# Local attention of a transformer kernel: three steps of 4, 4 and 3 query chunks per head pair in place of four of 3, 2, 3 and 3

## The reference, cut to what matters

```python
for i in range(6):
    x = attn_layer(shift_tokens(x), Wqkv[i], q_scale[i], k_scale[i], Wo[i]) + x
    x = ffn_layer(shift_tokens(x), ...) + x

def attn_layer(x, Wqkv, qs, ksc, Wo):
    q, k, v = split(x @ Wqkv)               # 16 heads of 64
    q, k = l2norm(q) * qs, l2norm(k) * ksc  # then rotary tables with a scale
    sim = 8 * q @ k.T                       # only keys 0 to 32 tokens back, in windows of 32
    return softmax(sim) @ v @ Wo
```

## Time and profile before

| | |
|---|---|
| Median of 3 runs | 5900.51 us (5897.06 to 5904.95) |
| Span of the profiled execution | 5900.4 us |
| Its own time beside the span | not given apart; the runs' median is 0.1 us above the span |
| PE busy | 5495.2 us, 93% |
| DVE busy | 4294.8 us, 73% |
| ACT busy | 4093.6 us, 69% |
| POOL busy | 2762.7 us, 47% |
| DMA queue 1 | 76.74 MB, 4.6% of 16 engines |

### The profile page before, as it was taken

The page is one execution under the profiler, slowest core; times in us unless marked ns, Lnnn a source line. Parts: engine busy times, 40 slices in busy tenths (PEclk is TensorE's granted clock), DMA queues, the critical chain, the costliest instruction groups (busy, mean ns, idle before and its releaser), DMA issues. The chain is left out here.

```text
span 5900.4 us, 159891 instructions
## 1 busy us (share of the span) xinstructions
PE 5495.2 (93%) x60258; PEld 3949.3 (67%) x60258; DVE 4294.8 (73%) x6692; ACT 4093.6 (69%) x7768; POOL 2762.7 (47%) x2483
## 2 busy tenths in 40 slices
PE   8998986899999999999998899899999999999998
PEld 3334443678777777777776333677777778777776
DVE  7876654777777777777775886777777777777775
ACT  5774654677777777777775577677777777777775
POOL 1101100566655665556663110566556666556663
PEclk8997998899999999999999899999999999999999
DMA  0000000100000000000000000100000000000000
GB/s 13 2 2 6 2 3 8 36 17 16 19 14 19 17 16 20 15 18 16 16 21 10 4 2 2 36 17 16 20 13 19 17 16 21 16 17 16 17 20 18
DMA packets 128857, 87.46 MB, mean 15 GB/s; under 512 B 33332, under 2 KB 121936, under 8 KB 128056
## 3 DMA queue, kind: packets, MB, share of 16 engines
q1 hardware_dynamic: 128056, 76.74, 4.6%
HBM read 68.96 MB, written 1.05 MB: 12 GB/s over the span
## 5 line engine op out<-in xcount | busy, mean ns | idle before, releaser
L1733 POOL TENSOR_TENSOR cross<-raw,tab_b 128x512 f32<-128x512 f32 x768 | 998.1, 1324 | 304.6 <-ACT raw L1600 301.8
L737 DVE TENSOR_REDUCE arena<-PS 128x1 f32<-128x512 f32 (+3 forms) x1408 | 828.4, 646 | 216.4 <-PE PS L550 130.5
L1739 POOL CAST kT_b<-kT 128x512 bf16<-128x512 f32 x384 | 311.9, 812 | 1318.2 <-ACT kT L1656 1318.2
L688 ACT ACTIVATE arena<-PS 128x1024 f32<-128x1024 f32 (+1 forms) x704 | 668.4, 968 | 203.1 <-PE PS L573 126.3
L1853 DVE TENSOR_TENSOR oT<-PS,rec_den 128x288 f32<-128x288 f32 (+1 forms) x768 | 326.2, 425 | 635.2 <-ACT rec_den L1634 635.2
L1824 DVE TENSOR_TENSOR rot<-PS,tab_a 128x512 f32<-128x512 f32 x768 | 521.9, 686 | 227.9 <-PE PS L1451 133.8
L1406 PE MATMUL PS<-qT,kT 64*128 64x96 f32 x8448 | 660.6, 287 | 0.0
L1626 ACT ACTIVATE PT<-PS 128x576 f32<-128x576 f32 (+1 forms) x768 | 468.7, 610 | 257.9 <-PE PS L1406 245.3
L1600 ACT COPY raw<-PS 128x512 f32<-128x512 f32 x768 | 447.1, 589 | 285.5 <-PE PS L1451 244.8
L1840 DVE TENSOR_TENSOR rot<-rot,cross 128x1024 f32<-128x1024 f32 x384 | 613.4, 1597 | 17.8 <-POOL cross L1733 17.4
L1847 DVE TENSOR_TENSOR rot<-rot,inv_norm 128x1024 f32<-128x1024 f32 x384 | 578.6, 1507 | 10.6
(11 more groups left out here) (260 smaller groups left out, 13084.0 us busy)
## 6 DMA issues: line engine op xcount, KB each, us to landing
w_qk<-in_w_pairs SPq DMA_DIRECT2D x196, 128.0 KB, 2.1
w_v<-in_w_pairs SPq DMA_DIRECT2D x100, 128.0 KB, 2.2
w_o<-in_w_out_pairs SPq DMA_DIRECT2D x192, 64.0 KB, 1.9
xs<-staged SPq DMA_DIRECT2D x24, 224.0 KB, 2.6
w<-in_L_ffn_W SPq DMA_DIRECT2D x12, 341.0 KB
q_parts<-max_rows SPq DMA_DIRECT2D x192, 2.0 KB
V<-in_c_E SPq DMA_DIRECT2D x2, 896.0 KB, 8.3
w<-in_L_ffn_W SPq DMA_DIRECT2D x24, 64.0 KB
```

Source lines behind the costliest of these rows:

```text
L688: nc.scalar.activation(PT[u % 6].rearrange("p (a n) -> p a n", a=2)[:, :, first_q:512], PS[:, 2 * (u % 2):2 * (u % 2) + 2, first_q:512], A ...
L737: nc.vector.tensor_reduce(maxima[:, 2 * m + h, qt, kh:kh + 1], bank[:, 0:keys_of(qt, kh)], AX.X, ALU.max).then_inc(bank_free, 1)
L1733: nc.gpsimd.tensor_tensor(dst[:, :, :, o:o + 32], src[:, :, :, other:other + 32], tab[:, :, o:o + 32].unsqueeze(2).broadcast_to([128, 8, 2 ...
```

## The change

Three steps of 4, 4 and 3 chunks take the place of four of 3, 2, 3 and 3. Tiles for exp and denominators grow to four chunks; the number of steps in the semaphore counts becomes NS = 3; the row group of a mask product is looked up for each chunk, since a step now has chunks of both. Slot 4 follows slot 3 with no step between them, on PE, ACT and DVE. The last step's values, denominators and quotient stay at the start of the next position.

```diff
-        PT = [own(f"PT{m}", [128, 2, 3 * QC]) for m in range(2)]
-        log_den = own("log_den", [128, 3 * QC])
-        rec_den = [own(f"rec_den{m}", [128, 3 * QC]) for m in range(2)]
+        PT = [own(f"PT{m}", [128, 2, 4 * QC]) for m in range(2)]
+        log_den = own("log_den", [128, 4 * QC])
+        rec_den = [own(f"rec_den{m}", [128, 4 * QC]) for m in range(2)]
...
-        STEPS = ((0, (0, 1, 2)), (0, (3, 4)), (1, (5, 6, 7)), (1, (8, 9, 10)))
+        STEPS = (range(0, 4), range(4, 8), range(8, 11))
+        NS = len(STEPS)
...
                 def scores(l, b, p, r, s):
-                    g, chunks = STEPS[s]
+                    chunks = STEPS[s]
...
-                    need(pe, exp_done, r * 4 + s)
+                    need(pe, exp_done, r * NS + s)
                     for i, c in enumerate(chunks):
+                        g = int(c in GROUPS[1])
...
@@ position of PE
                     if oo:
-                        values(r - 1, 3, (p + 6) % 8)
+                        values(r - 1, NS - 1, (p + 6) % 8)
...
-                    for s in range(3):
+                    for s in range(NS - 1):
                         if bb:
                             scores(l, b, p, r, s + 1)
...
                             values(r, s, (p + 7) % 8)
                         late(l, b, p, s + 2)
+                    late(l, b, p, 4)
...
@@ position of DVE
-                    for s in range(1, 4):
+                    for s in range(1, NS):
                         late(l, b, p, s + 1)
-                        if bb and s < 3:
+                        if bb and s < NS - 1:
                             quotients(r, s, (p + 1) % 2)
+                    late(l, b, p, 4)
```

More of the change, by code:

```diff
@@ L1423, in values @@
                 def values(r, s, pair):
-                    chunks = STEPS[s][1]
-                    need(pe, exp_done, r * 4 + (s + 1))
-                    need(pe, o_done, r * 4 + s)
+                    chunks = STEPS[s]
+                    need(pe, exp_done, r * NS + (s + 1))
+                    need(pe, o_done, r * NS + s)
                     for i, c in enumerate(chunks):
@@ L1455, in max_rows @@
                 def max_rows(l, b, p):
-                    need(pe, exp_done, (item(l, b, p) - 1) * 4)
+                    need(pe, exp_done, (item(l, b, p) - 1) * NS)
                     for g in range(2):
@@ L1466, in outputs @@
                     if f == 0:
-                        need(pe, o_done, (item(l, b, p) - 1) * 4)
+                        need(pe, o_done, (item(l, b, p) - 1) * NS)
                         need(pe, wo_in, (item(l, b, p) - 1) * 16)
@@ L1622, in exps @@
                 def exps(r, s):
-                    n = QC * len(STEPS[s][1])
-                    need(act, st_full, r * 4 + (s + 1))
-                    need(act, pv_full, r * 4 + (s - 1))
+                    n = QC * len(STEPS[s])
+                    need(act, st_full, r * NS + (s + 1))
+                    need(act, pv_full, r * NS + (s - 1))
                     nc.scalar.activation(PT[s % 2][:, :, 0:n], PS[:, 4:6, 0:n], ACT.Exp).then_inc(exp_done, 1)
                 def denominators(r, s):
-                    n = QC * len(STEPS[s][1])
-                    need(act, pv_full, r * 4 + (s + 1))
+                    n = QC * len(STEPS[s])
+                    need(act, pv_full, r * NS + (s + 1))
                     nc.scalar.activation(log_den[:, 0:n], PS[:, 7, 0:n], ACT.Ln).then_inc(ln_done, 1)
-                    need(act, ln_done, r * 4 + (s + 1))
-                    need(act, o_done, r * 4 + (s - 1))
+                    need(act, ln_done, r * NS + (s + 1))
+                    need(act, o_done, r * NS + (s - 1))
                     nc.scalar.activation(rec_den[s % 2][:, 0:n], log_den[:, 0:n], ACT.Exp, scale=-1.0).then_inc(den_done, 1)
@@ L1681, in position @@
                     if oo:
-                        denominators(r - 1, 3)
+                        denominators(r - 1, NS - 1)
                     if a:
@@ L1849, in quotients @@
                 def quotients(r, s, par):
-                    chunks = STEPS[s][1]
+                    chunks = STEPS[s]
                     lo, n = QC * chunks[0], QC * len(chunks)
-                    need(dve, den_done, r * 4 + (s + 1))
+                    need(dve, den_done, r * NS + (s + 1))
                     nc.vector.tensor_tensor(oT[par][:, lo:lo + n], PS[:, 6, 0:n], rec_den[s % 2][:, 0:n], ALU.mult).then_inc(o_done, 1)
@@ L1918, in position @@
                     if oo:
-                        quotients(r - 1, 3, p % 2)
+                        quotients(r - 1, NS - 1, p % 2)
                     if bb:
```

## The result

The changed kernel takes 5867.8 us (median; 5859.9 to 5870.5) against 5901.0: a ratio of 0.994, 95% interval 0.9926 to 0.9954, or 33 us less. I had forecast 100 us less. The sign and most terms of the sum were right; one wait was not in it, and one effect, the clock, was some fifteen times as large as I priced it.

A forecast was written before the change was run, and what follows sets the result against it. The prediction took PE, busy 93% of the span, as the bound. From about 5900 us it took 83 + 93 saved less 33, 13, 28 and 2 of new costs, 100 us: 5800 us, range 5740 to 5870.

The forecast's parts named there:

- Cheaper steps: On PE, three steps instead of four save a step's fixed part, 0.43 us a pair, 83 us over 192 pairs.
- Rival 3: Only what is removed is saved: just the ones product has a fixed part per step, 15 us; 5868 us, chance 0.12.
- Waits that go: PE's values products stop waiting for quotients (65 us) and mask products mostly for an exp (28 us): 93 us saved.
- (a): Slot 4: PE waits to turn K1 and q1 behind DVE's normalise, at positions 1, 2 and 4: 33 us lost.
- (b): Position 3: slots 3 and 4 back to back load ACT with copies, 0.6 us each time: 13 us lost.
- (c): Position 7: next batch's first query-key product waits 2.3 us for X1 at 12 places, loop returns already idle: 28 us lost.
- (d): Granted clock falls to half after one in eight of 12 gaps, 1.25 us each: 2 us lost.
- ACT loses an Exp, a Ln and an Exp per pair ... I cost it at nothing: ACT's and DVE's fewer instructions per pair shorten no path, because PE is the bound: 0 us.
- Waits that come: The prediction's list of new PE waits and their clock cost after the change, terms (a) to (d): 33, 13, 28 and 2 us.
- Rival 1: Slower: DVE's chain at slot 4 runs longer as the sine add stretches beside POOL; 5944 us at 1.2 us more, chance 0.08.
- rival 2: More gain: new waits (a), (b) and (c) overlap or don't come; 5725 us, chance 0.12.

The follow-up runs named there:

- four_again: Four steps of 3, 3, 3, 2 chunks put back in the changed kernel with the first two edits, sine's reorder and X1 turned in slot 2: 5929.9 us.
- sine: Changed kernel with the first two edits, plus DVE's sine add for the second half moved ahead of quotient 0: 5761.9 us, ratio 0.9759.
- stat: Changed kernel with ACT's two layer-norm rstd instructions moved from slot 4 of position 2 to slot 0 of position 3: 5813.6 us, ratio 0.9851.
- before_both: Kernel before, with its four steps, given the first two edits: 5888.8 us, ratio 0.9978.
- the first two edits: On the changed kernel, stat's rstd move, and Q0 and Q1 waiting for X0 alone (alone 5836.0 us); both together 5799.3 us.

## Why the prediction was right and wrong

- **Cheaper steps, 83 us:** right. 0.44 a pair, 84 us. The fixed part is in all four groups: in the medians the mask products take 0.44, 0.35 and 0.27 us for 4, 3 and 2 chunks, the scores 1.06, 0.84 and 0.62, the values 0.71, 0.55 and 0.38, the ones products 0.74, 0.59 and 0.42. That leaves some 0.09, 0.18, 0.05 and 0.1 beside the chunks, and four_again gives it back. Rival 3, that only the ones product has it, is out. The page "TensorEngine Tiling (Array Packing)" of the Trainium skill, section "Instruction Overhead", counts about 60 cycles for each matmul, and the estimate from it was 19 us, less than a quarter of what the rows show. That the rest comes from the changes between the groups' tile shapes is likely, but no run tried it.
- **Waits that go, 93 us:** right. 60 us at the values and 30 at the mask products.
- **(a) Turning K1 and q1, 33 us:** right in mechanism and about right in size. The profile has 27 us of idle time for it (47.0 less the 19.6 that was there), but a wait also costs the overlap with the product before it, 0.1 to 0.15 us. From start to start position 2 loses 0.5, position 4 0.75 and position 1 0.1, against 0.55, 0.8 and 0.15, and position 7 loses 0.45, which I had not listed: 1.8 x 22 = 40. sine shows the cause and gives 37 back.
- **(b) ACT's copies at position 3, 13 us:** about right in size. N1's product and the second maxima product of position 4 take 0.5 and 0.2 us more, 15 us; it was N1 and the banks after it that waited, and not Q0. No experiment tried it.
- **(c) X1, 28 us:** 12 gaps of 1.76, 21 us, with the 0.33 to 0.45 ahead of them counted under (a): the forecast 2.3 split in two. But I called the 8 loop returns hidden, and they grew by 1.0 us each: **8 us missed**.
- **(d) The clock, 2 us:** wrong, and by far. Slow stretches are in 19 places against 1 before, 7 at loop returns, 6 at X1 and 6 at position 3 behind the waits for banks. Over their 12 products each costs about 1.2 us (0.21 from start to start against 0.12, and a little more), 22 us, but the lower clock lasts on into the groups behind them. By all of PE's work it is (78 - 14) / 2 = 32 us: **30 us missed**. PE's busy time agrees, for it fell by only 50 us where the steps alone take 84 away. I had taken a share of one in eight from gaps of 2.2 us and used it for others. The share was misread too: I judged seven returns by their first product. In the kernel before, the clock fell at three of the eight, 1.4 us after PE had gone on at the second return of the earlier trace rows:

```profile
2110.52:2111.92 1.40, 1.40 (x12) 1.40 (x12) 0.47 (x1) 0.40 (x1) 0.00 (x0) 1.00 0.08 18
...
2112.00:2115.00 3.00, 3.00 (x20) 1.40 (x19) 1.97 (x3) 1.10 (x3) 2.76 (x1) 0.50 0.01 3
```

  By the changed kernel's trace half of the X1 gaps pay, and waits of 1.1 us behind another of 0.5 do too.
- **What was not in the sum:** the step "ACT loses an Exp, a Ln and an Exp per pair ... I cost it at nothing" looked at ACT's work and not at its queue. "Waits that come" walks through slot 4 for PE and DVE, and through ACT's copies only at position 3; it left out ACT's wait for DVE's moments at the head of slot 4 in position 2. **38 us missed**, shown by stat and by the control before_both.

The sum with measured terms is 84 + 90 - 37 - 15 - 21 - 8 - 32 - 38 = 23, against 33 measured. The 10 us that are left are not assigned; some terms are idle time and some are taken from start to start, and for (a) alone the two ways differ by 13 us. The forecast failed by the wait that it left out and by the clock. The time of 5867.8 lies inside my range and on rival 3's 5868 by chance: rival 3's mechanism was refuted, and the gain fell to its size for another reason. Rival 1 did not come (the sine add kept 1585 ns on the page), and rival 2 did not.

## What to carry to other kernels

When a step between two slots is taken out, read every engine's queue at the second slot for waits at its head, and ask what stands behind them: here a wait of an engine that was 69% busy cost 38 us, and 17 more by the clock. A step boundary costs the bound engine a fixed part and cover for everybody else; count both, and look again at orders that were right for the old number of steps, since the same swap gave 37 us with three steps and cost 51 with four. Removing a wait at a semaphore can leave the same delay one bank further on. And where a time moves more than its waits explain, read the granted clock behind them: of the 54 and 32 us that the first two edits gave, 17 and 22 were clock.

## What the runs showed of the hardware

The share of idle gaps after which the granted clock falls is no property of their length: of 12 identical gaps of 1.76 us, 6 were followed by some 2.5 us at 1.2 GHz in one kernel and 2 in another, and none where bf16 products filled them. The first product behind a gap doesn't tell either: at one return it ran at full pace, and the clock fell 1.4 us later. And the gap of PE at the return of a hardware loop was 1.9 to 4.0 us, in the mean 2.1 to 3.2, for programs that differ little around the jump.
